# Unread products on TensorE in the last attention steps and in the routing, with the last batch's low parts all on VectorE and its rows turned for the router directly

## The reference

```
x: (16, 112, 256)   ctx: (16, 375, 192)   16 heads of 16
x = x + tanh(g_xattn) * (softmax(q k^T / 4) v) Wo      q = layernorm(x) Wq, k = ctx Wk, v = ctx Wv
t = layernorm(x)
p = softmax(t router_w^T)       8 experts, the two best kept and divided by their sum
y = sum over the two experts of p_e * ((silu(t gate_e + gb_e) * (t up_e + ub_e)) down_e + db_e)
x = x + tanh(g_ffn) * y
```

## Time and profile before

| | |
|---|---|
| median of 3 runs | 561.27 us (557.2 to 562.57) |
| the profiled execution | 561.69 us, its span 559.9 us |
| TensorE busy | 475.1 us, 85% of the span |
| VectorE busy | 407.3 us, 73% |
| ScalarE busy | 324.5 us, 58% |
| GpSimd busy | 297.7 us, 53% |
| mean granted TensorE clock | 0.927 |
| attention ends, routing begins | at 318.7 us |
| first expert tile begins on TensorE | at 343.45 us |

### The profile page before, as it was taken

How to read it: one execution, slowest core, us unless ns; L and a number is a source line. 1 busy time by engine, 2 the same in 40 slices (tenths; PEclk the granted TensorE clock), 3 DMA queues, 4 the chain that set the end, 5 groups by cost and what they waited for, 6 DMA issues and landing times. The chain is left out here.

```text
span 559.9 us, 15117 instructions
## 1 busy us (share of the span) xinstructions
PE 475.1 (85%) x4723; PEld 433.4 (77%) x4724; DVE 407.3 (73%) x871; ACT 324.5 (58%) x625; POOL 297.7 (53%) x268
## 2 busy tenths in 40 slices
PE   2986999999999999999988524899899999999920
PEld 1875889998889988989877523698799999999820
DVE  5965889998999989999996486687865545555410
ACT  4642556676676567667555595677855455455510
POOL 5093466665557656655686206144657765654440
PEclk9988999999999999999997555899999999999975
DMA  8566677775567466555403296576734433433333
GB/s 210 148 164 149 158 186 179 185 185 125 136 160 188 108 174 182 131 155 113 99 13 109 70 355 213 186 232 198 142 51 75 73 51 66 66 52 51 39 39 131
DMA packets 69022, 74.88 MB, mean 134 GB/s; under 512 B 28744, under 2 KB 57248, under 8 KB 68784
## 3 DMA queue, kind: packets, MB, share of 16 engines
q1 hardware_dynamic: 60912, 63.23, 42.3%
q0 software_dynamic: 8064, 11.06, 12.1%
HBM read 42.51 MB, written 14.98 MB: 103 GB/s over the span
## 5 line engine op out<-in xcount | busy, mean ns | idle before, releaser
L366 POOL TENSOR_TENSOR PL<-PT 125x448 f16<-125x448 f32 x112 | 109.6, 986 | 104.9 <-ACT PT L499 104.8
L499 ACT ACTIVATE PT<-bank 125x448 f32<-125x448 f32 x192 | 100.9, 543 | 86.1 <-PE bank L630 85.8
L787 DVE TENSOR_REDUCE mx<-bank 112x1 f32<-112x375 f32 x256 | 125.0, 538 | 20.6 <-PE bank L612 19.4
L1242 POOL DMA_INDIRECT acc_scr<-ys,slot_row x42 | 67.0, 1595 | 81.7 <-ACT ys L1316 72.7
L630 PE MATMUL bank<-QS,KS 98*125 98x256 f32 x384 | 82.7, 305 | 4.4 <-DMA QS<-nm 3.4
L612 PE MATMUL bank<-KS,QS 97*112 97x376 f32 x256 | 80.3, 354 | 3.1 <-DMA KS<-bias_scr 1.6
L1569 DVE SCALAR_TENSOR_TENSOR hf<-bank,ub,sg 128x256 f32<-128x256 f32 x84 | 38.4, 482 | 49.7 <-ACT sg L1293 49.6
L1384 PE MATMUL bank<-xH,GH 128*128 128x256 f16 x336 | 65.7, 278 | 6.2 <-DVE xL L1548 3.6
L630 PEld LDWEIGHTS bank<-QS,KS 98*125 98x125 f32 x384 | 63.7, 193 | 6.2 <-DMA QS<-nm 2.9
L1384 PE MATMUL bank<-xL,GH 128*128 128x256 f16 x336 | 65.3, 277 | 0.3 <-issue 0.3
L1384 PE MATMUL bank<-xH,GL 128*128 128x256 f16 x336 | 65.1, 276 | 0.0
(11 more groups left out here) (218 smaller groups left out, 1045.4 us busy)
## 6 DMA issues: line engine op xcount, KB each, us to landing
KS<-kH SPq DMA_DIRECT2D x128, 94.0 KB, 2.2
KS<-kL SPq DMA_DIRECT2D x64, 94.0 KB, 2.2
QS<-q_scr SPq DMA_DIRECT2D x96, 56.0 KB
ctx_sb<-in_ctx SPq DMA_DIRECT2D x16, 281.2 KB
wsq<-in_L_ffn_gate_w SPq DMA_DIRECT2D x8, 512.0 KB, 3.7
wsq<-in_L_ffn_up_w SPq DMA_DIRECT2D x8, 512.0 KB, 4.5
w_raw<-in_L_ffn_gate_w SPq DMA_DIRECT2D x8, 512.0 KB
w_raw<-in_L_ffn_up_w SPq DMA_DIRECT2D x8, 512.0 KB
```

What stands on the lines that cost most here:

```text
L366: pool.tensor_tensor(PL[:, 2 * k:2 * k + 2, :, 0:N], PT[:, 2 * k:2 * k + 2, :, 0:N], PH[:, 2 * k:2 * k + 2, :, 0:N], ALU.subtract).then_in ...
L499: act.activation(PT[:, 2 * k:2 * k + 2, :, 0:N].rearrange("p a e i -> p (a e) i"), psST[k % 2][0:JP].rearrange("p (a i) -> p a i", i=NI)[: ...
L787: dve.tensor_reduce(mx[:, hd:hd + 1], psS[hd % SBANKS][0:N, 0:M], AX.X, ALU.max).then_inc(v_max, 1)
L1242: pool.indirect_dma_start(acc_scr, bass.IndirectOffsetOnAxis(ap=slot[:, TH * t + k:TH * t + k + 1].bitcast(U32), axis=0), ys[:, u, k, :], ...
```

## The change

Four edits.

1. **Unread products.** A helper `idle` issues `count` transposes of the identity matrix into a PSUM bank that nobody reads at that time. It is called with 2 in each of the first 12 slots of step 17, with 6, 2 and 3 in step 18 (ahead of `out_T`, behind it, and behind `project_o`), with 2 in step 19 (behind `center_T`), and in the routing with 26 after the product of squares, 26 after the turned biases and 30 after the table. That makes 37 in the attention and 82 in the routing.
2. **Low parts.** In step 17 all 12 low parts of batch 15 are made by VectorE (`ends`, `on_pool`); `sums` waits for VectorE's count alone. VectorE's semaphore counts 12 for that batch.
3. **Direct turn.** For batch 15 `center_T` turns X itself, once its residual is added (it waits for v_x1), and no longer xc (it waited for a_mean). The copy to xcT then has a factor of 1.
4. **One wait less.** For batch 15 `variances` doesn't wait for the turn before it overwrites xc.

```diff
--- before.py
+++ after.py
@@ -75,6 +75,11 @@
         banks = [whole.enter_context(nc.psum_tensor(f"bank{i}", [128, 512], F32)) for i in range(6)]
         misc = whole.enter_context(nc.psum_tensor("misc", [128, 1024], F32))
         psS, psST, psO = [banks[0], banks[1], banks[5]], banks[2:4], banks[4:6]
+
+        def idle(pe, bank, count):
+
+            for n in range(count):
+                pe.transpose(bank[:, 0:128], ident[:], ident[:])
 
         attention(nc, locals())
         experts(nc, locals())
@@ -191,6 +196,9 @@
 
         heads_at = {0: (0,), 1: (1, 2, 3), 2: (4, 5), 4: (6, 7), 5: (8, 9), 6: (10, 11), 7: (12, 13, 14), 8: (15,)}
 
+        ends = lambda i, c: isinstance(i, int) and NB * i + c == B + 1
+        on_pool = lambda i, c, k: k in POOL and not ends(i, c)
+
         SBANKS = len(psS)
         KP = (1, 2)
         VP = (5, 6, 7)
@@ -228,6 +236,10 @@
         def live(i, c, back):
 
             return not isinstance(i, int) or 0 <= NB * i + c - back < B
+
+        def direct(b):
+
+            return isinstance(b, int) and b == B - 1
 
         def starts(i, c):
 
@@ -402,7 +414,7 @@
 
                 def step(i, c):
                     for k in range(SLOTS):
-                        if k in POOL and live(i, c, 2):
+                        if on_pool(i, c, k) and live(i, c, 2):
                             low(i, c, k)
                         if k == VR and live(i, c, 1):
                             values(i, c)
@@ -457,7 +469,8 @@
                 def variances(i, c):
 
                     b, h, u = at(i, c - 4)
-                    act.wait_ge(p_xc, b + 1)
+                    if not direct(b):
+                        act.wait_ge(p_xc, b + 1)
                     act.wait_ge(a_mean, b + 1)
                     act.activation(xc[:], X[:, bass.ds(b, 1), :].rearrange("i o d -> i (o d)"), ACT.Square,
                                    bias=mv2[:, bass.ds(b, 1), 0:1].rearrange("i o d -> i (o d)"),
@@ -473,7 +486,7 @@
                             act.wait_ge(p_xc, b + 1)
                             wait(act, p_lg, b)
                             act.activation(xcT[:], psS[1][:, 0:2 * N].rearrange("p (c i) -> p c i", c=2), ACT.Copy,
-                                           scale=-float(DIM)).then_inc(a_xc, 1)
+                                           scale=1.0 if direct(b) else -float(DIM)).then_inc(a_xc, 1)
                         if k == AG and live(i, c, 4):
                             variances(i, c)
                         if k == SQ and squared(i, c) is not None:
@@ -640,8 +653,12 @@
                     if p % 4 == 0:
                         wait(pe, v_os, 2 * b + p // 4)
                     k = last_bank(p)
-                    pe.wait_ge(v_L, vec(SB - 1) * b + vec(k))
-                    pe.wait_ge(g_L, pol(SB - 1) * b + pol(k))
+                    if ends(i, c):
+                        pe.wait_ge(v_L, vec(SB - 1) * b + k + 1)
+                        pe.wait_ge(g_L, pol(SB - 1) * b)
+                    else:
+                        pe.wait_ge(v_L, vec(SB - 1) * b + vec(k))
+                        pe.wait_ge(g_L, pol(SB - 1) * b + pol(k))
                     for e in range(2):
                         hd = 2 * p + e
                         for part, P in enumerate((PH, PL)):
@@ -662,12 +679,16 @@
 
                 def center_T(i, c):
                     b, h, u = at(i, c - 4)
-                    pe.wait_ge(a_mean, b + 1)
+                    if direct(b):
+                        pe.wait_ge(v_x1, b + 1)
+                    else:
+                        pe.wait_ge(a_mean, b + 1)
                     wait(pe, v_lg, b)
                     if live(i, c, 1):
                         pe.wait_ge(v_nm, b + 4)
                     for k in range(2):
-                        mm = pe.transpose(psS[1][:, N * k:N * (k + 1)], xc[:, 128 * k:128 * (k + 1)], ident[0:N, 0:N])
+                        rows = X[:, b, 128 * k:128 * (k + 1)] if direct(b) else xc[:, 128 * k:128 * (k + 1)]
+                        mm = pe.transpose(psS[1][:, N * k:N * (k + 1)], rows, ident[0:N, 0:N])
                     mm.then_inc(p_xc, 1)
 
                 def route(i, c):
@@ -692,6 +713,11 @@
                         return
                     slots(i, c)
 
+                def ahead(i, c, step, count):
+
+                    if isinstance(i, int) and NB * i + c == step:
+                        v["idle"](pe, psS[2], count)
+
                 def slots(i, c):
                     for s in range(SLOTS):
                         heads = heads_at.get(s, ()) if live(i, c, 1) else ()
@@ -699,6 +725,8 @@
                             scores_T(i, c, s)
                         if s in KP and live(i, c, 0):
                             project_k(i, c, KP.index(s))
+                        if s < SB and isinstance(i, int) and NB * i + c == B + 1:
+                            v["idle"](pe, psS[2], 2)
                         for hd in heads[0:1]:
                             scores(i, c, hd)
                         if s in pv_at and live(i, c, 2):
@@ -710,13 +738,17 @@
                         if s == MT and live(i, c, 1):
                             max_T(i, c)
                         if s == OT and live(i, c, 3):
+                            ahead(i, c, B + 2, 6)
                             out_T(i, c)
+                            ahead(i, c, B + 2, 2)
                         if s == OP and live(i, c, 3):
                             project_o(i, c)
+                            ahead(i, c, B + 2, 3)
                         if s == CT and live(i, c, -1) and not starts(i, c):
                             ctx_T(i, c + 1)
                         if s == XT and live(i, c, 4):
                             center_T(i, c)
+                            ahead(i, c, B + 3, 2)
                         if s == LG and live(i, c, 4):
                             route(i, c)
 
@@ -829,7 +861,7 @@
                         heads = heads_at.get(s, ()) if live(i, c, 1) else ()
                         for hd in heads[0:1]:
                             maximum(i, c, hd)
-                        if 0 < s <= SB and s - 1 not in POOL and live(i, c, 2):
+                        if 0 < s <= SB and not on_pool(i, c, s - 1) and live(i, c, 2):
                             low(i, c, s - 1)
                         if s == KP[-1] + 1 and live(i, c, 0):
                             key_low(i, c)
@@ -1323,6 +1355,7 @@
                 pe.wait_ge(q_k, 1)
 
                 pe.matmul(bN[:, 0:E], ones[:], sq[:], start=True, stop=True).then_inc(t_n, 1)
+                v["idle"](pe, bI, 26)
                 pe.wait_ge(q_k, 4)
                 pe.wait_ge(e_both, 1)
                 flat = both[:].rearrange("i b e -> i (b e)")
@@ -1348,6 +1382,7 @@
                                        chunks[:, k, b].rearrange("i w h -> i (w h)")[:, 0:(1 + k) * NH],
                                        start=(k == 1 and b == 0), stop=(k == 0 and b == B - 1))
                 mm.then_inc(t_tab, 1)
+                v["idle"](pe, bN, 30)
 
                 kept = {}
 
```

## The result

The changed kernel takes 556.1 us (median of 20 runs, 553.74 to 558.88), where the kernel before took 560.31 us in the same rounds (20 runs, 557.2 to 562.57). The ratio is 0.9927 with a 95% interval of 0.9913 to 0.9941: 4.1 us less (3.3 to 4.9). That is a gain clear of noise, and smaller than the 1% that the prediction used as its bound.

A forecast was written before the change was run, and what follows sets the result against it. It took half-clock TensorE to bound most of step 17, after waits for GpSimd's low parts. Gains of 3.1 + 0.9 + 1.1 = 5.1 us gave 556.6 from the profiled 561.69, forecast as 556.2 us for the median; range 553.5 to 565.5.

The forecast's parts named there:

- The sum, 556.2 us: Whole kernel: gains of 3.1, 0.9 and 1.1 us in the attention's last three steps, 5.1 us in all.
- Step 17, 3.1 us less: Attention: VectorE's queue, with all twelve low parts at 0.63 us, ends at 308.80 us instead of 311.91.
- With the products kept at the full clock: Attention, step 17: unread products keep TensorE at full clock, so VectorE bounds the step; 3.1 us less.
- Step 18, 0.9 us less: Attention: at full clock the turn to ScalarE's copy takes 0.24 us less, the output projection to the residual 0.68 less.
- Step 19, 1.1 us less: Attention's end: direct turn and full clock cut residual to logits' copy from 2.63 to 1.49 us; 0.5 less at half clock.
- the three behind the projection delay only batch 14's logits, for which nobody waits: Attention, step 18: three unread products behind the output projection cost nothing on the path.
- Routing, nothing: Routing: its 82 products lie in waits of 5.05, 5.80 and 6.84 us at full clock and are worth about nothing.
- ScalarE's 5.33 us: After the routing's first turn: ScalarE's unnamed wait from 347.90 us hides any gain in first turn and first tile.
- Rival 1: Attention and routing: clock falls despite the products, which are paid; 4.2 us slower, 565.5 us; chance 0.20.
- Rival 2: Attention: one clock fall in step 18 or 19, or late in 17, gives back 1.5 to 3 us; 558.5 us; chance 0.15.
- Rival 3: TensorE ahead of the first tile: 119 more products cause an instruction fetch, giving back 5.33 us; 561.5 us; chance 0.07.
- Rival 4: Experts' second tile: clock holds there too, 24 matmuls in 2.62 not 4.37 us, 1.7 us more; 554.5 us; chance 0.08.

The follow-up runs named there:

- The kernel with ten products: Changed kernel with only 10 unread products left (6 and 2 in step 18, 2 in step 19), none in the routing; ratio 0.9927 to the kernel before.
- the last experiment: Changed kernel with 10 unread products in the attention, 26, 26 and 56 in the routing, 8 behind the first tile's turn; 554.28 us, ratio 0.9925.

## Why the prediction was right or wrong

**The sum, 556.2 us: right, 556.1 measured.** That it is right to 0.1 us is luck. The sum took 5.1 us off a median of three runs, 561.27; with 20 runs the kernel before has 560.31, and the gain is 4.1 us (3.3 to 4.9). A start that was 1.0 us too high and a gain that was 1.0 us too large cancelled. Of the three terms, 3.1, 0.9 and 1.1 us, the typical profiles show 3.1, nothing and 0.7.

**Step 17, 3.1 us less: right in size, wrong in cause.** The queue of VectorE laid end to end gave 10.63 us, and that is what was measured. Two errors cancelled. Back to back the low parts start every 0.57 us, not every 0.63: the nine and the three of the kernel without products take 5.20 and 1.60 us from their first to the instruction behind them, 6.8 together instead of 7.56, and that is the whole way from 10.63 to 9.86 us. And the products, which I laid beneath VectorE's time since TensorE had 7.5 of 10.6 us to do, cost 0.8 us. The failed step is that comparison of totals: TensorE works in order, and the products stood ahead of the unit for which ScalarE waited. Free time in the sum is not free time at that place in the queue.

**"With the products kept at the full clock": the failed reason.** I saw that GpSimd's four slow low parts stood ahead of the fall, and gave the merit to the products. With the low parts moved and no product in the step the clock held in four of five profiles, and that edit gives 3.9 us; the products alone give 2.9; together they give 3.85.

**Step 18, 0.9 us less: true of the profile that it was read from, not of the kernel.** In two further profiles of the kernel before the clock is back by step 18, and nothing is won there.

**Step 19, 1.1 us less: 0.7 measured.** The step that failed is "the three behind the projection delay only batch 14's logits, for which nobody waits". `center_T` waits for them, since they lie in the same PSUM bank. The rows of TensorE in the changed kernel, projection, three products, logits, turn:

```profile
308.66 0.40 PE L707 MATMUL bank<-wo_h,oTL 128*112 128x256 f32 x2
308.89 0.49 PE L82 MATMUL bank<-ident 128*128 128x128 f32 x3
309.22 0.47 PE L698 MATMUL bank<-rwT,xcT 128*112 128x8 f32 x4
310.04 0.38 PE L691 MATMUL bank<-ident,XW 112*128 112x112 f32 x2 [0.35 <-DVE routed L892]
```

The turn could have started at 309.57, the end of the residual, and started at 310.04, and ScalarE's copy of it followed at 310.46, 0.89 us after the residual where 0.58 was predicted. The kernel with ten products lacks those three. Its residual ends at 312.67:

```profile
312.89 0.38 PE L691 MATMUL bank<-ident,XW 112*128 112x112 f32 x2 [0.44 <-DVE routed L889]
...
313.31 0.36 ACT L488 ACTIVATE xcT<-bank 128x224 f32<-128x224 f32 x1
...
313.72 0.56 PE L698 MATMUL bank<-rwT,xcT 128*112 128x8 f32 x4 [0.23 <-ACT xcT L488]
...
314.32 0.17 DVE L889 COPY routed<-bank 112x8 f32<-112x8 f32 x1 [1.57 <-PE bank L698]
```

There the copy comes 0.64 us after the residual, close to the 0.58, and step 19 took 2.14 us instead of 2.39. So 0.25 us of the missing 0.4 are the three products, 0.06 the copy of batch 14's logits, for which the turn waits in any case, and 0.1 the last piece: from the logits' matmuls to their copy it takes 0.60 us, where I had estimated 0.5.

**Routing, nothing: right, and not at the full clock that it was laid out with.** The kernel without its 82 products has the same steps and the same first tile. The clock fell to 0.50 twice in the changed kernel's routing, from 314.3 to 317.7 and from 321.1 to 324.5 us, the first time while the products ran. Each group of 26 took 4.5 to 4.6 us, not 2.9, and still found room. The reason that I gave for the first tile, ScalarE's 5.33 us, was of one execution. In the others the first tile at half clock is on the path, and there the change simply leaves it: the products end at 332.9 us, and the first turn comes at 337.95.

**Rival 1, the clock falls in step 17 and the products are paid: didn't happen**, in none of the profiles with products in that step. With it falls the rule of the Trainium skill ("TensorE: Matmul & The Clock Gate", Part 4) that transposes don't count as activity. The changed kernel's routing has a stretch in which TensorE has nothing but them, from 321.52 us. Here it is in stretches of 1 us:

```profile
321.50:322.50 1.00, 1.00 (x6) 0.98 (x6) 1.00 (x7) 0.86 (x3) 0.00 (x0) 0.50 1.23 473
322.50:323.50 1.00, 1.00 (x7) 1.00 (x6) 0.96 (x3) 1.00 (x5) 0.00 (x0) 0.50 0.91 361
323.50:324.50 1.00, 1.00 (x6) 1.00 (x6) 1.00 (x2) 1.00 (x5) 0.00 (x0) 0.50 0.93 379
324.50:325.50 1.00, 1.00 (x11) 1.00 (x10) 1.00 (x1) 1.00 (x4) 0.00 (x0) 0.99 1.05 368
```

The clock comes back while only turns of the identity run, and the number of matmuls in each goes from 6 or 7 to 11. In the kernel without any product the clock stays at 0.50 from 312 to 345 us. For these float32 turns the measurement decides against the page.

**Rival 2, a fall for a part:** it was the kernel before that had it, as its first profile against the other two shows; and one of the five without products in step 17. **Rival 3, fetching instructions:** not seen; the routing takes as long with 82 products more as without. **Rival 4:** there was nothing to win. The second tile's half clock came with the 5.33 us wait of the first profile; in both kernels' other profiles 48 matmuls on either side of the second tile's start take 5.24 us, 2.62 for each 24. What can be had is the first tile's clock, as the last experiment shows.

**The chances.** Within 1% was given 0.57 and came. The thin margin to "faster by over 1%" was stated; even the whole 5.1 us of the sum would have been 0.9%.

## What to carry to other kernels

When a clock falls, look first for the engine whose slow work makes TensorE wait ahead of the fall; giving that work to an engine that sits idle may keep the clock and shorten the step too (3.9 us here), where filler products only keep the clock (2.9 us). Neither is shown to keep it in every execution. Filler has a price where it stands ahead of work that someone waits for: put it in front of a wait that is known to be long, as the ten products of steps 18 and 19 stand (2.14 us for step 19, 2.72 without any). And profile the kernel before more than once: a stretch that is up to chance can put a us into the estimate that the change has nothing to do with, as step 18 did, and time it more than three times, since a base of three runs was off by as much.

## What the runs showed of the hardware

Transposes of the identity bring the granted clock from 0.50 to 1.00 by themselves, at 324.5 us of the changed kernel (above). The same instructions of step 17 ran at full clock in four kernels' profiles and at half clock for 6.8 us in a fifth (299.6 to 306.4 us); TensorE was busy 6.40 of 6.40 us in that stretch, so that being busy in the profile's sense did not bring the clock back at once. In the routing the clock even fell while TensorE ran products without a gap (from 313.0 us, with 0.68 us of work in the two us before; 0.50 from 314.3). And a low part is slower on VectorE beside GpSimd's: 0.59 us with GpSimd idle, 1.09 us beside it.
